# Forty products of zeros on TensorE in the set-up of an attention block kernel

## The reference

```python
h = group_norm(hidden_states, norm_gamma, norm_beta)      # 32 groups of 16 channels
q = conv1x1(h, wq, bq)
k = conv1x1(h, wk, bk)
v = conv1x1(h, wv, bv)
attn = jnp.einsum('bci,bcj->bij', qf, kf) * scale          # 1024 x 1024 per image
attn = jax.nn.softmax(attn, axis=2)
out = jnp.einsum('bcj,bij->bci', vf, attn).reshape(B, C, H, W)
out = conv1x1(out, wo, bo)
return residual + out
```

## Time and profile before

| | |
|---|---|
| median of 3 runs | 2145.7 us (2145.09 to 2147.06) |
| the profiled execution: first to last instruction | 2145.2 us |
| its PE busy | 2121.6 us, 99% |
| its DVE, ACT, POOL busy | 1381.5, 673.7, 192.5 us |
| mean granted clock of TensorE | 0.997 |
| HBM traffic | 38.02 MB read, 33.55 MB written |

### The profile page before, as it was taken

The page is one execution under the profiler, slowest core; times in us unless marked ns, Lnnn a source line. Parts: engine busy times, 40 slices in busy tenths (PEclk is TensorE's granted clock), DMA queues, the critical chain, the costliest instruction groups (busy, mean ns, idle before and its releaser), DMA issues.

```text
span 2145.2 us, 25470 instructions
## 1 busy us (share of the span) xinstructions
PE 2121.6 (99%) x9328; PEld 1753.5 (82%) x9328; DVE 1381.5 (64%) x2219; ACT 673.7 (31%) x1113; POOL 192.5 (9%) x92
## 2 busy tenths in 40 slices
PE   6999999999999999999999999999999999999999
PEld 5878888888888888888888888888888888888887
DVE  6466584756757567575675847658475685756746
ACT  3241322413334132332413224132241333324232
POOL 1010100101000010010100101010000100001000
PEclk9999999999999999999999999999999999999999
DMA  3102001020110202001020010200102020010101
GB/s 123 40 1 79 1 31 50 1 79 1 41 39 1 79 1 80 1 12 67 1 80 1 20 59 0 80 1 36 44 1 79 1 79 1 9 71 1 40 0 40
DMA packets 31520, 73.33 MB, mean 34 GB/s; under 512 B 4640, under 2 KB 4640, under 8 KB 31392
## 3 DMA queue, kind: packets, MB, share of 16 engines
q1 hardware_dynamic: 29136, 71.31, 9.1%
q10 hardware_dynamic: 2256, 0.27, 0.1%
HBM read 38.02 MB, written 33.55 MB: 33 GB/s over the span
## 4 chain that ended last, share of the span: by engine, by line
PE 97%; issue 1%; POOL 1%; DMA 0%; DVE 0%; SPq 0%; ACT 0%; POOLq 0%; DVEq 0%
PE bank L243 32%; PE bank L244 32%; PE bank L245 32%; DMA xt<-in_wv 0%; POOL p_lo L207 0%; POOL all_max L212 0%; POOL rstd L217 0%; POOL all_max L227 0%; SPq L174 0%; SPq L173 0%; DVE stage L686 0%; DVE stage L680 0%; DVE run_max L651 0%; DVE h_lo L558 0%; DVE t_lo L642 0%
## 5 line engine op out<-in xcount | busy, mean ns | idle before, releaser
L243 PE MATMUL bank<-t_hi,h_hi 128*128 128x512 f32 x1024 | 399.3, 390 | 3.0 <-DVE t_lo L642 2.9
L245 PE MATMUL bank<-t_hi,h_lo 128*128 128x512 f32 x1024 | 398.8, 390 | 0.0
L244 PE MATMUL bank<-t_lo,h_hi 128*128 128x512 f32 x1024 | 398.8, 389 | 0.0
L243 PE MATMUL bank<-p_hi,v_hi 128*128 128x512 f32 x1024 | 398.3, 389 | 0.0
L244 PE MATMUL bank<-p_lo,v_hi 128*128 128x512 f32 x1024 | 398.3, 389 | 0.0
L245 PE MATMUL bank<-p_hi,v_lo 128*128 128x512 f32 x1024 | 398.3, 389 | 0.0
L444 ACT COPY scores<-bank 128x512 f32<-128x512 f32 x256 | 145.9, 589 | 397.7 <-PE bank L245 397.3
L448 ACT ACTIVATE scores<-scores 128x512 f32<-128x512 f32 x256 | 159.8, 628 | 325.1 <-DVE scores L656 325.0
L243 PEld LDWEIGHTS bank<-t_hi,h_hi 128*128 128x128 f32 x1024 | 192.6, 188 | 43.9 <-issue 3.3
L651 DVE TENSOR_TENSOR run_max<-run_max,scores 128x512 f32<-128x512 f32 x192 | 132.9, 692 | 146.9 <-ACT scores L444 142.9
L244 PEld LDWEIGHTS bank<-t_lo,h_hi 128*128 128x128 f32 x1024 | 192.7, 188 | 39.9
(11 more groups left out here) (83 smaller groups left out, 2715.1 us busy)
## 6 DMA issues: line engine op xcount, KB each, us to landing
out<-stage SPq DMA_DIRECT2D x128, 256.0 KB, 2.1
xt<-in_x SPq DMA_DIRECT2D x15, 2048.0 KB, 8.1
xt<-in_x SPq DMA_DIRECT2D x4, 512.0 KB, 12.1
scores<-in_wk SPq DMA_DIRECT2D x4, 256.0 KB, 5.0
scores<-in_wq SPq DMA_DIRECT2D x4, 256.0 KB, 5.2
xt<-in_wo SPq DMA_DIRECT2D x1, 1024.0 KB, 8.1
xt<-in_wv SPq DMA_DIRECT2D x1, 1024.0 KB, 10.6
stage<-in_bv ACTq DMA_DIRECT2D x1, 256.0 KB, 13.1
```

The source lines that it names most:

```text
L243: nc.tensor.matmul(o, a_hi, b_hi, start=start, stop=False)
L244: nc.tensor.matmul(o, a_hi, b_lo, start=False, stop=False)
L245: return nc.tensor.matmul(o, a_lo, b_hi, start=False, stop=stop)
```

## The change

A new helper `filler` issues products of one tile with itself. The tile is the first quarter of `t_hi`, set to zero by a new memset that is DVE's first instruction. The results go to banks which no one reads before they are overwritten (each product starts its own sum). Twelve run ahead of the first weight product, once the memset is done; twenty-eight run between the last weight product and the first image, once `wkq_split` has reached 4. Eight of these have 128 weight columns and 512 streamed ones, eight 96 and 512, six 128 and 256, six 128 and 384.

```diff
--- before.py
+++ after.py
@@ -146,8 +146,8 @@
             sem(n) for n in ("bq_step", "bv_used", "diagonals_set", "biases_set"))
         t_split, v_split, h_split, p_split = (sem(n) for n in ("t_split", "v_split", "h_split", "p_split"))
         max_step, centred, sum_step, inv_set = (sem(n) for n in ("max_step", "centred", "sum_step", "inv_set"))
-        zeros_set, bn_set, chan_set, group_step, var_set, scale_step, h_full = (
-            sem(n) for n in ("zeros_set", "bn_set", "chan_set", "group_step", "var_set", "scale_step", "h_full"))
+        filler_set, zeros_set, bn_set, chan_set, group_step, var_set, scale_step, h_full = (
+            sem(n) for n in ("filler_set", "zeros_set", "bn_set", "chan_set", "group_step", "var_set", "scale_step", "h_full"))
         o_scaled, o_done = sem("o_scaled"), sem("o_done")
 
         block = ctx.enter_context(nc.Block())
@@ -247,6 +247,13 @@
             def cols(n):
                 return slice(n * P, (n + 1) * P)
 
+            def filler(times, o, m, n):
+
+                for _ in range(times):
+                    nc.tensor.matmul(o[0:m, 0:n], t_hi[:, 0, 0:m], t_hi[:, 0, 0:n], start=True, stop=True)
+
+            pe.wait_ge(filler_set, 1)
+            filler(12, bank[7], P, HALF)
 
             for o in range(KC):
                 pe.wait_ge(wk_split, o + 1)
@@ -273,6 +280,12 @@
                     mm = product(bank[4 + c][:], wv_hi[:, o, cols(c)], wv_lo[:, o, cols(c)],
                                  wot_hi[:, o, :], wot_lo[:, o, :], o == 0, o == KC - 1)
                 mm.then_inc(wov_summed, 1)
+
+            pe.wait_ge(wkq_split, KC)
+            filler(8, bank[0], P, HALF)
+            filler(8, bank[0], 96, HALF)
+            filler(6, bank[0], P, 256)
+            filler(6, bank[0], P, 384)
 
             def t_part(half, c, k):
                 q = slice(half * HALF, (half + 1) * HALF)
@@ -558,6 +571,7 @@
                 nc.vector.tensor_tensor(h_lo[:, k, q], scores[:, slot, :], h_hi[:, k, q].bitcast(F32),
                                         ALU.subtract).then_inc(h_split, 1)
 
+            nc.vector.memset(t_hi[:, 0, :].bitcast(F32), 0.0).then_inc(filler_set, 1)
             nc.vector.memset(chan[:], 0.0).then_inc(zeros_set, 1)
             nc.vector.memset(square[:], 0.0).then_inc(zeros_set, 1)
```

## The result

| | before | with the change |
|---|---|---|
| median of 19 runs each | 2145.24 us (2143.64 to 2147.63) | 2149.38 us (2148.25 to 2150.81) |
| ratio | | 1.0018, 95% interval 1.0011 to 1.0025 |
| the profiled execution, span | 2145.2 us | 2146.5 us |

The change costs 4.1 us, 0.2%; the interval of the ratio is +2.4 to +5.4 us. The forecast was 2149.1 us.

What follows compares the result with a forecast made beforehand. The prediction took the tensor engine as the bound, busy 2121.6 of 2145.2 us. It added 0 for the start filler and +3.4 us for the late one to a median of 2145.7: 2149.1 us, range 2146.4 to 2152.0.

Steps and rivals of the forecast that it cites:

- The late filler starts behind the fourth `wkq_lo`: Before the first image: the filler waits for DVE's last subtraction, ending at 40.54 us, and starts at 40.60 us.
- Its length: Late filler before the first image: 23.5 full-size products, over at 47.5 to 48.9 us depending on the clock's rise.
- The image at full clock: First image's first stage: its 48 products run at full clock behind the filler, taking 10.9 us.
- The stage: First image's first stage: ends at 58.8 us instead of 55.96, +2.9 us (+2.5 to +3.9).
- Which rise belongs to the median: Restart at 42.07 us: slowest rise in the median run gives +2.9 us, the middle one +3.9; +3.4 taken.
- The start filler is worth 0: Program start: twelve products speed nine weight products by 1.8 us, but a later PE wait takes it all; worth 0.
- Nothing swallows the delay: After the first image's first stage: later work and the stall before 113.42 us move along; the delay reaches the end whole.
- the rival: Stall before 113.42 us: it uses up PE's delay, leaving +0 to +0.5 us, 2146.0 us; chance 0.07.
- Zeros do not wake the clock: Late filler: products of zeros leave the clock at half, +7.3 to +8.7 us, 2153.7 us; chance 0.09.
- The filler in the gap: Idle before the first image: filler over at 38.5 us, image starts warm, -2.9 us, 2142.8 us; chance 0.04.

Runs made afterwards that it cites:

- e3: The changed kernel with its twenty-eight late products waiting for one increment of `wkq_split` instead of four: 2145.15 us against 2145.28 for the unchanged kernel.
- e2: The changed kernel without the twelve products at the start, late twenty-eight and memset kept: 2149.34 us against 2145.28 for the unchanged kernel.
- e1: The changed kernel without the twenty-eight late products, only the memset and the twelve at the start: 2145.17 us against 2145.28 for the unchanged kernel.
- e5: The changed kernel with the late filler issued twice (56 products): 2155.06 us against 2145.62 for the unchanged kernel.
- e6: The changed kernel with only three late products (128x512) instead of twenty-eight: 2144.89 us against 2145.62 for the unchanged kernel.
- e7: The changed kernel with the late filler reading real weights (`wkq_hi`) instead of zeros: 2149.86 us against 2145.62 for the unchanged kernel.
- e4: The changed kernel with thirty-six 128x512 products behind one `wkq_split` increment in place of the late twenty-eight: 2142.94 us against 2145.28 for the unchanged kernel.
- e8: e4 without the twelve products at the start: 2143.39 us against 2145.62 for the unchanged kernel.

## Why the prediction was right

The mechanism, the start at 40.6, the place of the cost and its whole way to the end stood as forecast. That 2149.1 stands only 0.3 us from the 2149.38 measured is in part luck: the cost was taken 0.7 us too small, and the 2145.7 that it was added to, a median of three runs, was 0.5 us above the 2145.24 of the nineteen.

- *The late filler starts behind the fourth `wkq_lo`.* It ended at 40.88 us instead of 40.54, and the filler started 0.06 us later, at 40.94. The 0.3 us are POOL's, whose `rstd` came 0.3 us later. e3 shows it from the other side: the same products behind one increment start at 32.6 us and cost nothing.
- *Its length.* Forecast 6.9 us for a rise after 3.1 us; the profile has 3.2 us and 7.0 us to the image's first product. For a rise after 6.1 us the forecast was 8.3; e2 has 5.9 us and 8.3 us to the image's first product at 49.13.
- *The image at full clock.* Forecast 10.9 us for its 48 products; 47.95 to 58.87 is 10.9.
- *The stage.* Forecast +2.9 against the profiled execution; +2.91. That it fell on the centre has some luck in it: the filler started 0.3 us late, and the rise was 0.8 us quicker than the 4.0 assumed.
- *Which rise belongs to the median.* The text left it open between +2.9 and +3.9 and took +3.4; the measured difference is 4.1. Restart to full clock took, in the seven profiles with a slow restart there: 6.1 (before), 3.2 (the change), 2.9 (e1), 5.9 (e2), 3.6 (e5), 3.1 (e6) and 6.2 us (e7), 4.4 in the mean, with nothing between 3.6 and 5.9. With 4.4 us in both kernels the forecast's own working gives 48.1 + 10.9 = 59.0 after and 42.07 + 0.16 + 10.9 + 9.9 x 0.2 = 55.1 before: +3.9 us. So, as far as the medians tell, the step that was mis-sized is the half taken back by trusting before's profile, which was a slow draw. The interval of the measured difference, +2.4 to +5.4 us, holds both +3.4 and +3.9; but the two other versions with the same late filler, e2 and e7, have +4.1 and +4.2. The Trainium skill, "TensorE: Matmul & The Clock Gate" (Part 1), says that the number of slow products varies between runs of one kernel; going by it alone would have given +3.9. These seven numbers are in line with it, though each comes from another kernel; the nearest to a test is e2 against the change, the same late filler with 5.9 and 3.2 us.
- *The start filler is worth 0.* e1 shows it (-0.1 us), and e4 and e8 differ by no more than their scatter. The reason was only half right in its detail. In the profile of the change there was no pause behind the twelve: they ran at half speed almost to the end (5.3 us, as forecast), and the first weight product followed them directly. In e1 the wait ahead of the wov products grew to 1.0 us, as forecast. In the profile of the change it shrank to 0.19 us, because DVE's row was itself 1.1 us earlier in that execution, and PE idled 9.0 instead of about 7.5 us before the late filler. e4's profile has 0.25 us in the same way. Either way PE then waits for `rstd`.
- *Nothing swallows the delay.* The stall before 116.01 is still 2.57 us long, where the rival needed it nearly gone, and what follows up to image 1 is no shorter behind a late start than behind an early one. e5 doubles the filler and its median has the second lot's 5.3 us in full. What the clock does in the stall at 113 us is absorbed, as e1's second wait shows.
- *Zeros do not wake the clock*: refuted by the profile, and e7 shows no difference to data.
- *The filler in the gap*: did not happen in the change. Tried in e3, it is worth 0 rather than up to 2.9 us, because of the fall after the idle time; e4 and e8 get 2.2 to 2.3 us of it by a filler that reaches almost to the image.

## What to carry to other kernels

A filler that keeps TensorE's clock up must run while the engine has nothing to do; ask which semaphore lets it start, and whether that event is the same one that ends the gap. Behind such an event only the slack to the first real product is free (here 1.5 us, three products), and all the rest is added to the time. It must also reach nearly to the real work: the one that ended 4 us ahead gained nothing, those that ended 0.6 and 1.5 us ahead gained 2.2 to 2.3 us, 0.1% of this kernel. Before costing a slow restart from one profile, look at several: here it took 2.9 to 6.2 us, and the one profile shown before the change was nearly the worst.

## What the runs showed of the hardware

- The granted clock can fall after PE is back at work: in e3 it outlasted 3.95 us of idle and fell 0.6 us after the restart, for 3.4 us. With 1.45 us of idle (e4) and 0.59 us (e8) it did not fall.
- Nor does the length of the idle time alone tell what comes. The stall of 2.4 to 2.9 us within the image ended in three ways: slow from its first product on (before, 2.90 us of idle), fast throughout (e1, 2.40 us), and in e2, after 2.48 us, fast at first and slow from 118.66 us, 1.6 us after the restart:

```profile
117.09 0.49 PE L243 MATMUL bank<-t_hi,h_hi 128*128 128x512 f32 x1 [2.48 <-DVE t_lo L655]
...
118.66 0.63 PE L243 MATMUL bank<-t_hi,h_hi 128*128 128x512 f32 x1
```

- The clock column says 1.00 from the start of the program, yet the first products in before were 0.43 us apart; the level before the first recorded change must be read from the spacing.
- POOL's wait ahead of `rstd`, for nothing the profile shows, moves the start of the image by about 1 us between profiles. It is not a wait for DVE: `var_g`, its input, was complete at 30.58 us in before and at 27.69 us in the change, 2.9 us earlier, and `rstd` still started 0.3 us later. POOL's timeline of e4:

```profile
37.72 1.05 POOL L217 TENSOR_TENSOR rstd<-var_g,minus_half 128x4 f32<-128x4 f32 x1 [6.67 <-issue]
```

and of e6:

```profile
38.52 1.05 POOL L217 TENSOR_TENSOR rstd<-var_g,minus_half 128x4 f32<-128x4 f32 x1 [7.75 <-issue]
```

The Trainium skill, "GPSIMD Engine Reference", (2.1, instruction dispatch) says that the first call of freshly loaded code costs about 6 us that no instruction in the profile shows. The waits here, 6.7 to 7.8 us ahead of `rstd`, which follows another kind of operation on POOL each time, would fit with that; no run took the switch away, so the cause is not shown. This wait makes up most of the gap of 9 us in which PE idles, and was not part of this change.
